# Feed-forward of a decoder layer: the last tile kept on chip, and a ring of loads laid over the matmul input by blocks

## What is computed

```
x = act_qdq(x)
up = act_qdq(x @ lpbq_dequant(w_up).T)
gate = act_qdq(x @ lpbq_dequant(w_gate).T)
sig = fixed_qdq_u16(jax.nn.sigmoid(gate))
gate = act_qdq(gate * sig)
o = act_qdq(gate * up)
return o @ lpbq_dequant(w_down).T
```

## Time and profile before

| | |
|---|---|
| median of 3 runs | 3564.81 us (3563.89 to 3568.51) |
| the profiled execution | 3561.65 us |
| its span in the trace | 3559.7 us |
| PE busy | 3233.0 us, 91% of the span |
| DVE, ACT busy | 2578.7 us, 2279.3 us |
| moved by DMA | 555.47 MB, mean 156 GB/s |

### The profile page before, as it was taken

One profiled execution on the slowest core, in us unless ns is written; L12 is line 12 of the kernel. 1 busy time (PEld: TensorE's weight loads), 2 busy tenths in 40 slices (PEclk: granted clock), 3 DMA queues, 4 the chain that ended last, 5 costly groups with the idle time before them and its releaser, 6 DMA issues.

```text
span 3559.7 us, 47086 instructions
## 1 busy us (share of the span) xinstructions
PE 3233.0 (91%) x15056; PEld 2498.3 (70%) x15056; DVE 2578.7 (72%) x4060; ACT 2279.3 (64%) x4138; POOL 1076.8 (30%) x1177
## 2 busy tenths in 40 slices
PE   5899999999999999977999999988989999941998
PEld 4777777777787878765666666655768888831887
DVE  5887777777777777756787878877963369876564
ACT  4786766666676767644777777766442256678765
POOL 1223232323333333333655655656500000000000
PEclk9999999999999999988999999999999999975999
DMA  3344433433443443327575656664712268889764
GB/s 119 137 152 139 127 125 116 149 115 125 131 134 113 134 135 117 113 71 137 110 127 114 121 115 126 120 99 152 252 74 107 107 216 296 288 332 397 274 244 183
DMA packets 269955, 555.47 MB, mean 156 GB/s; under 512 B 28025, under 2 KB 105857, under 8 KB 255377
## 3 DMA queue, kind: packets, MB, share of 16 engines
q1 hardware_dynamic: 265488, 544.08, 51.8%
q10 hardware_dynamic: 4224, 8.39, 0.6%
HBM read 322.72 MB, written 162.30 MB: 136 GB/s over the span
## 4 chain that ended last, share of the span: by engine, by line
PE 39%; DVE 6%; issue 5%; DMA 2%; ACT 1%; POOL 1%; SPq 0%; DVEq 0%; ACTq 0%; POOLq 0%
PE gu_acc L2436 15%; PE ca_mx L2351 3%; PE md_acc L2516 2%; PE md_acc L2517 2%; PE md_acc L2518 2%; DVE ca_negm L1953 2%; PE ca_pj L2331 2%; PE ca_ov L2381 2%; PE ca_ov L2382 2%; PE ca_st L2369 2%; PE ca_pj L2318 2%; DVE ca_el L1968 1%; PE ca_ms L2341 1%; DMA ca_q<-ca_ql 1%; DVE ca_eh L1962 1%
## 5 line engine op out<-in xcount | busy, mean ns | idle before, releaser
L816 POOL TENSOR_SCALAR sa_ex<-sa_ex,sa_rs 128x512 f32<-128x512 f32 x512 | 356.9, 697 | 939.6 <-DVE sa_rs L658 939.6
L653 DVE TENSOR_REDUCE sa_nm<-sa_st 128x1 f32<-128x512 f32 x512 | 351.6, 687 | 274.2 <-PE sa_st L941 273.0
L514 ACT ACTIVATE sa_eh<-sa_tr 128x512 fp32r<-128x512 f32 x512 | 306.8, 599 | 294.5 <-PE sa_tr L951 291.2
L898 PE MATMUL sa_pj<-sa_xh,sa_w 128*128 128x512 f32 x1536 | 456.9, 417 | 22.9 <-DVE sa_kl L636 11.1
L507 ACT ACTIVATE sa_ex<-sa_st,sa_nm 128x512 f32<-128x512 f32 x512 | 351.1, 686 | 59.7 <-DVE sa_nm L653 56.9
L1953 DVE TENSOR_REDUCE ca_negm<-ca_mx 128x2 fp32r<-128x1024 f32 x256 | 312.7, 1222 | 100.8 <-PE ca_mx L2351 97.1
L662 DVE TENSOR_TENSOR sa_el<-sa_tr,sa_eh 128x512 fp32r<-128x512 f32 x512 | 351.5, 686 | 39.0 <-ACT sa_eh L514 32.1
L2225 POOL TENSOR_TENSOR ca_el<-ca_ex,ca_eh 128x512 fp32r<-128x512 f32 x256 | 352.4, 1378 | 59.7 <-ACT ca_eh L1737 59.4
L1729 ACT ACTIVATE ca_ex<-ca_st 128x512 f32<-128x512 f32 x512 | 296.4, 586 | 40.0 <-PE ca_st L2369 38.5
L898 PEld LDWEIGHTS sa_pj<-sa_xh,sa_w 128*128 128x128 f32 x1536 | 262.3, 190 | 68.4 <-issue 26.5
L951 PE MATMUL sa_tr<-top_ident,sa_ex 128*128 128x128 f32 x2048 | 306.3, 272 | 0.7 <-POOL sa_ex L816 0.7
(11 more groups left out here) (292 smaller groups left out, 7510.8 us busy)
## 6 DMA issues: line engine op xcount, KB each, us to landing
sa_w<-w_split SPq DMA_DIRECT2D x56, 1536.0 KB, 7.5
gate<-gu_ev SPq DMA_DIRECT2D x24, 1024.0 KB, 4.4
gu_g<-gate SPq DMA_DIRECT2D x48, 512.0 KB, 5.8
gate<-gu_g SPq DMA_DIRECT2D x48, 512.0 KB, 3.5
up<-gu_ev SPq DMA_DIRECT2D x24, 1024.0 KB, 5.7
md_a<-gate SPq DMA_DIRECT2D x96, 256.0 KB, 6.8
md_b<-up SPq DMA_DIRECT2D x96, 256.0 KB, 7.4
md_a<-gate SPq DMA_DIRECT2D x44, 512.0 KB, 15.3
```

The costliest lines, as they stand in the source:

```text
L514: nc.scalar.activation(eh[:, v % 2], tr[:, v % 2], ACT.Copy).then_inc(act_eh, 1)
L653: nc.vector.tensor_reduce(nm[:, u % U:u % U + 1], st[:, u % 2], AX_X, ALU.max, negate=True).then_inc(dve_mx, 1)
L816: nc.gpsimd.tensor_scalar(ex[:, u % U], ex[:, u % U], rs[:, u % U:u % U + 1], 1.0, ALU.mult, ALU.mult).then_inc(pool_n, 1)
L898: yield nc.tensor.matmul(pj[:, bank], w[:, n % 2, m, part, k], xx[:, b % 2, k], start=(i == 0 and k == 0), stop=(i == 2 and k == DK - 1))
```

## The change

- `xn3`, `xh` and `xl` are stored block by block (`[P, B, DK, S]`), and `da` and `db` become one ring `dab` whose slot i (8 KB per partition) lies over block i of `xh`. The first load into slot i waits only until the last round has finished block i.
- Tile 11 of silu and of up is no longer stored, nor loaded in the down stage; `quantise_chunk` reads it from `g_buf` and `ev`. So product loads are 11 a group, and they are numbered without it.
- `g_buf` must stay whole to the end. `xb` moves into the unused second halves of the ring's slots; `d_w_raw` moves behind `g_buf`, into free memory, and `d_wd` takes its old place.
- `load_down(0)` is issued at the end of round 22; the others stand before pieces 14, 26 and 38. `load_x2(0)` stands before chunk 6.

```
-            da = down("a", [P, DRING, W2])
-            db = down("b", [P, DRING, W2])
+            dab = down("ab", [P, DRING, 2, W2])
...
-            xb = down("xb", [P, 2, NT, D])
+        xb = [dab[:, NT * i:NT * i + NT, 0, S:W2] for i in range(2)]
...
                 if i >= DRING:
                     e.wait_ge(act_q, 2 * (m - DRING) + 2)
-                elif i == 0:
-                    e.wait_ge(u_pe_acc, B * ROUNDS)
+                else:
+                    e.wait_ge(u_pe_acc, B * (ROUNDS - 1) + i + 1)
...
             def load_product(i):
                 g, k = i // FT, i % FT
+                if k == FT - 1:
+                    return
+                i = (FT - 1) * g + k
                 c = (LOADED + i) % DRING
                 at = slice(g * S, (g + 1) * S)
                 if i >= DRING:
-                    e.wait_ge(act_dq, 2 * (i - DRING) + 2)
+                    before = i - DRING
+                    e.wait_ge(act_dq, 2 * (before + before // (FT - 1)) + 2)
...
-                if i == FT - 1:
-                    for h in range(2):
-                        e.wait_ge(u_out[h], 16 * ROUNDS)
-                    for n in range(PIECES):
-                        e.wait_ge(g_out[n], 16 * FT)
...
-                    if r == ROUNDS - 1 and n == PIECES - 1:
-                        break
+                    if r == ROUNDS - 1:
+                        continue
                     if j >= 0:
                         u_store_silu(j, n)
                     if n % 2:
                         u_store(r, n // 2)
-
-            u_store(ROUNDS - 1, 1)
+                if r == ROUNDS - 2:
+                    load_down(0)
             for h in range(2):
                 e.wait_ge(u_out[h], 16 * (ROUNDS - 1))
             for n in range(PIECES):
                 e.wait_ge(g_out[n], 16 * (FT - 1))
             for m in range(PIECES, TOTAL):
-                if m == PIECES + 2:
-                    load_down(0)
-                if m == PIECES + 4:
-                    u_store_silu(FT - 1, PIECES - 1)
-                if m >= EACH and m % EACH == 0:
+                if m % EACH == 2 and m > EACH:
                     load_down(m // EACH)
                 load_piece(m)
             for i in range(FCHUNKS):
-                if i == 3:
+                if i == 6:
                     load_x2(0)
...
             def quantise_chunk(i):
...
+                if k == FT - 1:
+                    one = g_buf[:, g // 2, g % 2 * S:(g % 2 + 1) * S]
+                    two = ev[:, g // HB, g % HB * S:(g % HB + 1) * S]
...
                     for k in range(DK):
-                        last = nc.tensor.matmul(u_acc[:, b % BANKS], ww[:, r % 2, k], xx[:, k, b * S:(b + 1) * S],
+                        last = nc.tensor.matmul(u_acc[:, b % BANKS], ww[:, r % 2, k], xx[:, b, k],
```

More of the change, by code:

```diff
@@ L1174, in cross_attention_and_feed_forward_stage @@
                 new = lambda name, shape, dt=F32: later.enter_context(nc.sbuf_tensor(f"ca_{name}", shape, dt))
-                xn3 = new("xn3", [P, DK, T])
+                xn3 = new("xn3", [P, B, DK, S])
                 cast_r = new("cast_r", [2 * HS, P], F32R)
@@ L1213, in cross_attention_and_feed_forward_stage @@
             gate("spare", [P, SPARE])
-            xh = gate("xh", [P, DK, T], F32R)
-            xl = gate("xl", [P, DK, T], F32R)
+            xh = gate("xh", [P, B, DK, S], F32R)
+            xl = gate("xl", [P, B, DK, S], F32R)
             g_buf = gate("g", [P, PIECES, W2])
@@ L1244, in cross_attention_and_feed_forward_stage @@
                 half = lambda name, shape, dt=F32: first_half.enter_context(nc.sbuf_tensor(f"md_{name}", shape, dt))
-                d_w_raw = half("w_raw", [P, FF])
+                d_wd = half("wd", [P, FF])
                 d_deq = Dequant(nc, half, FF, d_dve_q)
@@ L1248, in cross_attention_and_feed_forward_stage @@
                 half("g", [P, PIECES, W2])
-                d_wd = half("wd", [P, FF])
+                half("above_g", [P, 16])
+                d_w_raw = half("w_raw", [P, FF])
             oh2 = down("oh", [P, DR, S], F32R)
             ol2 = down("ol", [P, DR, S], F32R)
-            xb = down("xb", [P, 2, NT, D])
             d_acc = life.enter_context(nc.psum_tensor("md_acc", [P, 2, NT, D], F32))
+        xb = [dab[:, NT * i:NT * i + NT, 0, S:W2] for i in range(2)]
         c2, c3 = c23[:, 0, 0:1], c23[:, 1, 0:1]
@@ L1409, in cross_attention_and_feed_forward_stage @@
         turned = d_acc[:, 1]
-        tokens = lambda b: (slice(None), slice(None), slice(b * S, (b + 1) * S))
         def piece(m):
@@ L1558, in load_piece @@
                     e.wait_ge(act_q, 2 * (m - DRING) + 2)
-                elif i == 0:
-                    e.wait_ge(u_pe_acc, B * ROUNDS)
+                else:
+                    e.wait_ge(u_pe_acc, B * (ROUNDS - 1) + i + 1)
                 at = slice(n * W2, (n + 1) * W2)
-                e.dma_start(da[:, i % DRING], env["gate"][j, :, at]).then_inc(ab_in[i % DRING], 16)
-                e.dma_start(db[:, i % DRING], env["up"][j, :, at]).then_inc(ab_in[i % DRING], 16)
+                e.dma_start(dab[:, i % DRING, 0], env["gate"][j, :, at]).then_inc(ab_in[i % DRING], 16)
+                e.dma_start(dab[:, i % DRING, 1], env["up"][j, :, at]).then_inc(ab_in[i % DRING], 16)
             def load_down(j):
@@ L1574, in load_product @@
                 if i >= DRING:
-                    e.wait_ge(act_dq, 2 * (i - DRING) + 2)
+                    before = i - DRING
+                    e.wait_ge(act_dq, 2 * (before + before // (FT - 1)) + 2)
                 else:
                     e.wait_ge(act_q, 2 * (TOTAL - DRING + i) + 2)
-                if i == FT - 1:
-                    for h in range(2):
-                        e.wait_ge(u_out[h], 16 * ROUNDS)
-                    for n in range(PIECES):
-                        e.wait_ge(g_out[n], 16 * FT)
-                e.dma_start(da[:, c, 0:S], env["gate"][k, :, at]).then_inc(ab_in[c], 16)
-                e.dma_start(db[:, c, 0:S], env["up"][k, :, at]).then_inc(ab_in[c], 16)
+                e.dma_start(dab[:, c, 0, 0:S], env["gate"][k, :, at]).then_inc(ab_in[c], 16)
+                e.dma_start(dab[:, c, 1, 0:S], env["up"][k, :, at]).then_inc(ab_in[c], 16)
             def load_x2(g):
@@ L1590, in load_x2 @@
                     e.wait_ge(act_q, 2 * TOTAL)
-                e.dma_start(xb[:, g % 2], x2_rows[g]).then_inc(xb_in[g % 2], 16)
+                e.dma_start(xb[g % 2], x2_rows[g]).then_inc(xb_in[g % 2], 16)
             def out_loads(i):
@@ L1756, in high_input @@
                 e.wait_ge(dve_xq, b + 1)
-                nc.scalar.activation(xh[tokens(b)], qi[:, b % 2], ACT.Copy).then_inc(act_xh, 1)
+                nc.scalar.activation(xh[:, b], qi[:, b % 2], ACT.Copy).then_inc(act_xh, 1)
             def evict(r, b):
@@ L1809, in out_work @@
                         e.wait_ge(pe_st, U * N)
-                    nc.scalar.activation(xn3[:, :, cols(j)], pt(j).rearrange("p (k t) -> p k t", t=P),
+                    nc.scalar.activation(xn3[:, j // NT, :, cols(j % NT)], pt(j).rearrange("p (k t) -> p k t", t=P),
                                          ACT.Copy).then_inc(act_xo, 1)
@@ L1879, in quantise_piece @@
                     e.wait_ge(ab_in[c], 32 * ((m - PIECES) // DRING) + 32)
-                    one, two = da[:, c], db[:, c]
+                    one, two = dab[:, c, 0], dab[:, c, 1]
                 nc.scalar.activation(aq[:, m % 4], one, ACT.Abs, scale=ssc.inverse[:, 0:1]).then_inc(act_q, 1)
@@ L1884, in quantise_chunk @@
             def quantise_chunk(i):
-                c = (LOADED + i) % DRING
-                e.wait_ge(ab_in[c], 32 * ((LOADED + i) // DRING) + 32)
+                g, k = i // FT, i % FT
                 if i >= DR:
                     e.wait_ge(dve_oq, i - DR + 1)
-                nc.scalar.activation(daq[:, i % DR], da[:, c, 0:S], ACT.Copy, scale=ssc.inverse[:, 0:1]).then_inc(act_dq, 1)
-                nc.scalar.activation(dbq[:, i % DR], db[:, c, 0:S], ACT.Copy, scale=usc.inverse[:, 0:1]).then_inc(act_dq, 1)
+                if k == FT - 1:
+                    one = g_buf[:, g // 2, g % 2 * S:(g % 2 + 1) * S]
+                    two = ev[:, g // HB, g % HB * S:(g % HB + 1) * S]
+                else:
+                    l = LOADED + (FT - 1) * g + k
+                    e.wait_ge(ab_in[l % DRING], 32 * (l // DRING) + 32)
+                    one, two = dab[:, l % DRING, 0, 0:S], dab[:, l % DRING, 1, 0:S]
+                nc.scalar.activation(daq[:, i % DR], one, ACT.Copy, scale=ssc.inverse[:, 0:1]).then_inc(act_dq, 1)
+                nc.scalar.activation(dbq[:, i % DR], two, ACT.Copy, scale=usc.inverse[:, 0:1]).then_inc(act_dq, 1)
             def high_product(i):
@@ L1901, in store_y @@
                 e.wait_ge(dve_y, g + 1)
-                e.dma_start(y_rows[g], xb[:, g % 2]).then_inc(y_out[g % 2], 16)
+                e.dma_start(y_rows[g], xb[g % 2]).then_inc(y_out[g % 2], 16)
```

(6 more changed lines are left out.)

## The result

| | before | changed |
|---|---|---|
| median | 3564.80 us (7 runs) | 3554.28 us (7 runs) |
| profiled execution | 3561.65 us, span 3559.7 | 3556.59 us, span 3554.6 |
| ratio | | 0.9967 (0.9958 to 0.9977) |

A forecast was written before the change was run, and what follows sets the result against it. The pass for the product's maximum, paced by DMA loads while TensorE idles, was taken as the bound; ending it 11.7 us sooner takes the 3564.81 us median to 3553.1 us, range 3545 to 3560.

The forecast's parts named there:

- The sum: Pass: from 3171.5 DMA owes 36.25 MB, 93.0 us, plus 3.3; ScalarE ends at 3269.9 instead of 3281.6, 11.7 us less.
- The 3.3 us kept for latency and gaps: Load stream of the pass: latency and small gaps found in the kernel before, 3.3 us, kept unchanged in the forecast.
- rival (a): Restarted stream runs dry at pieces 14, 26 and 38: 4 to 8 us less gain, 3557 to 3561; 15%.
- Dropped stores: Pass: 1.5 MB of last-tile stores leave the load stream, 3.8 us; the early first down weights take out another 1.9 us.
- DMA under the last round: Last up round: prefetch beside TensorE's matmuls costs nothing; 1.6 us if they were a tenth slower.
- Loads in the down stage: Down stage: the 16 dropped product loads of tile 11 were hidden beside TensorE, so worth 0 on the path.
- Gate piece (11,2): End of round 22: queued behind the early weights, lands near 3137; cost zero, one microsecond at most.
- The block layout: xn3, xh and xl by blocks, with strided output writes at the start of gate: zero, with 1 us either way.
- A hole of 117 us leaves that alone: Start of down stage: TensorE's lower clock for the first six down matmuls, 0.43 us apart, stays as it was.
- (b): Pass: ScalarE becomes the bound at 106.8 us and a microsecond or two; gain 17 to 19, 3545 to 3548; 8%.
- (c): Pass: stream runs slower, gain gone at 2.89 us a MB, 363 GB/s; nothing gained, 3562 to 3567; 8%.
- (d): Down stage: chunk 24 lands later and TensorE stalls at each of six groups; slower, 3571 at 3 us each; 5%.

The follow-up runs named there:

- the repetition: The changed kernel measured once more, unedited, beside the kernel before on one chip: median 3552.08 us, ratio 0.9967 to before, pass 114.8 us.
- experiment 3: Changed kernel with the last tile's six stores (4 MB) put back behind the first eight pair loads, nothing read from them: ratio 0.9967, pass 114.6 us.
- experiment 4: Changed kernel with the last tile's stores put back and all 96 chunks loaded again in the down stage: ratio 0.9971, pass 115.1 us.

## Why the prediction was right

**What bounds.** That the pass is the stretch where time can be had, and that it passes on one for one, held: in the profiles of before and change the first down matmul follows the end of the pass by 5.29 and 5.30 us, and TensorE has no wait after it. In the medians 10.5 us, in the pass 10.3; in the repetition 14.6 and 11.4. The medians' difference thus moves by 4 us from one set of runs to another, and that the first came so near the forecast 11.7 is in part luck; the firmer figure is the pass.

**The sum.** The pass was to fall from 126.1 to 114.4 us. It fell to 115.9, and to 114.8 in the two other profiles. The stream was to resume at 3171.5; with the 4.0 us of this execution taken off, SP issued the second weights at 3171.7. The last piece was waited for until 3269.3 on that scale instead of 3267.8; in the other two it was 0.4 us late.

What the sum lacked is at the restart. It took pieces 12 and 13 as landed when the second weights are issued. In fact the DMA engines moved 257 GB/s from 3169.98 to 3175.67, 1.4 of these 2 MB, and the slowest of their four loads took 6.9 us from issue to landing; 0.6 MB, 1.6 us of DMA, was still owed (0.5 MB in the repetition). Then they ran at 341 and 348 GB/s over 8 us, 1.3 us short of 409. The 3.3 us kept for latency and gaps covered most of this, since they held 1.7 us of the same kind from the start of the stream before (263 GB/s from 3151.82 to 3155.50, 377 to 3160). The repetition came back sooner:

```profile
3165.41:3169.01 3.60, 0.00 (x0) 0.00 (x0) 3.60 (x5) 3.60 (x5) 0.00 (x0) 0.50 0.67 223
3169.01:3173.01 4.00, 1.67 (x8) 1.70 (x9) 4.00 (x6) 3.28 (x5) 0.00 (x0) 0.50 0.92 320
3173.01:3177.01 4.00, 1.12 (x6) 0.72 (x4) 2.30 (x5) 4.00 (x6) 0.00 (x0) 0.50 0.99 395
```

From 10.4 to 30 us behind ScalarE's start it moved 0.3 MB more, 0.8 us of the 1.1 between the two profiles; the rest is not accounted for. That is rival (a) in small, at one place of the three that it named; the waits before pieces 26 and 38 left no gap (409 to 416 GB/s in every 4 us from 3192 to 3260).

**The parts.** Dropped stores 3.8 us and weights 1.9 were measured as 4.5 and 1.4, by one profile each and without the prefetch; whether the early weights matter beside it was not tested. The prediction's remark that 12.25 MB less are begun 19.7 us later is the point of the case: eight MB prefetched (20.5 us of DMA) gave 4.4 to 5.5 us. The credit for the 1.5 MB of stores is real only where the stream is continuous; with the prefetch, experiment 3 shows it at nothing. The sum came out right because it counted from the restart, where the stores no longer appear.

**Costed at nothing.** DMA under the last round: 411 GB/s and matmuls unmoved. Loads in the down stage: experiment 4. Gate piece (11,2) behind the weights: ScalarE quantised it at 3141.68, which is 3137.69 on the old scale, against 3137.70 before. The block layout: TensorE's wait at the start of gate was 8.4 us against 9.0, within the microsecond set aside for it.

**The clock at the start of the down stage.** "A hole of 117 us leaves that alone" was wrong by 1.2 us: 12 gaps of 0.43 us in place of 6. Nothing shows it to be an effect of the change. Over the twelve profiles the number of such gaps was 6 before, 12 and 14 in the changed kernel, 6, 7, 8, 8, 11 and 12 in its variants without idle matmuls, and 0 in the three with them. The variants with 6 and with 12 differ only in DMA, but with one profile of the kernel before an effect of the change is not excluded. In the nine without idle matmuls the time from the first down matmul to the end was 271.4 us plus 0.2 for each gap, within 0.2. Which number an execution gets, nothing here tells.

**The rivals.** (b): ScalarE's bound is at 108.7 us, 6 to 7 us below the change, so the chance for it needed a faster stream than there is. (a) as the Trainium skill would size it ("DMA: Bandwidth & Descriptors", Anatomy of one DMA): that section gives its 2 us for DMAs issued from GpSimd, and these come from SP. The first 512 KB behind the hole landed 3.9 us after issue, with its pair behind it, against the estimate of 3.2 for a piece alone; the last piece came 0.4 to 1.5 us late in all, so there were no two or three gaps of 2 to 3 us. (c): the loads, with no store among them, ran at 410 GB/s from 3215 to 3260; the 358 GB/s of the Trainium skill ("DMA: Bandwidth & Descriptors", Where 436 GB/s comes from) does not bind one core here. The stretch before that the prediction set against it, from 3151.82 to 3279.55, took 127.7 us, not 126. (d): no wait of TensorE inside the down stage in any run.

## What to carry to other kernels

Where a stream of loads bounds a stretch, count what it owes and from which moment it runs without a break; a prefetch into a ring buys the time of the ring's bytes, less the time by which the rest of the stream then starts later, at the first free slot (20.5 - 14.8 us here). Before paying in code for fewer transfers, look whether the engine that moves them has a hole at that point: here the stores that were dropped would have cost nothing behind the prefetch. And when executions differ upstream by more than the effect, compare the stretch in the profiles, beside the medians.

## What was not expected of the hardware

After the hole the DMA engines needed some 10 to 14 us to come back to 409 GB/s: 212, 323, 342 and 391 GB/s in the four stretches from 3169.86 in the changed kernel's first profile, and 223, 320, 392 to 395 and 414 to 420 in the two others. It was not for want of loads alone: 0.6 of the first 2 MB had not been moved when SP issued the next at 3175.67. The same issues behind 4 MB of stores ran at 404 and 407. Why is not shown. And TensorE's first down matmuls came at the lower clock for 6 to 14 gaps in executions with the same work ahead of them, and for none after twelve idle ones that took 4.35 us.
